# A GRU scan over four directions: the border exchanged in four pieces, and fourteen homes for the last tiles

## The reference

```
seq = gn(x) @ Wi.T + bi                  # 192 -> 64 channels per pixel
r = sigmoid(xr + hr); z = sigmoid(xz + hz); n = tanh(xn + r * hn)
h_new = (1 - z) * n + z * h              # 128 steps along rows or columns
out = hs @ Wo.T + bo                     # 64 -> 192 channels
result = x + (right + down + left + up) / 4
```

## Time and profile before

| | |
|---|---|
| median of three runs | 2590.5 us (2584.61 to 2591.54) |
| profiled execution: own time, span | 2584.67 us, 2582.6 us |
| granted TensorE clock, mean | 0.989 |
| busy share of the span | TensorE 87%, VectorE 79%, ScalarE 62%, GpSimd 59% |
| DMA, mean over the span | 197 GB/s, 509.23 MB |

### The profile page before, as it was taken

The page is one execution under the profiler, slowest core; times in us unless marked ns, Lnnn a source line. Parts: engine busy times, 40 slices in busy tenths (PEclk is TensorE's granted clock), DMA queues, the critical chain, the costliest instruction groups (busy, mean ns, idle before and its releaser), DMA issues.

```text
span 2582.6 us, 79658 instructions
## 1 busy us (share of the span) xinstructions
PE 2255.1 (87%) x30544; PEld 1419.1 (55%) x30544; DVE 2053.0 (79%) x4910; ACT 1602.1 (62%) x3374; POOL 1534.0 (59%) x2108
## 2 busy tenths in 40 slices
PE   0679999999979999898979999899979999999886
PEld 0345555555546655555546665555546666555564
DVE  8239999777769999787859999788857777898854
ACT  0236666666657777666647777666657777666600
POOL 2026666667756666566656666566667766666600
PEclk9999999999989999999989999999999999999999
DMA  9973333246768786589977776589974544244299
GB/s 364 276 213 94 99 94 87 79 133 207 244 196 232 209 228 181 157 241 281 311 249 204 216 233 173 156 248 278 308 228 127 129 130 116 79 127 129 60 381 390
DMA packets 331354, 509.23 MB, mean 197 GB/s; under 512 B 36704, under 2 KB 145632, under 8 KB 330208
## 3 DMA queue, kind: packets, MB, share of 16 engines
q1 hardware_dynamic: 313248, 478.28, 63.3%
q10 hardware_dynamic: 17728, 25.85, 2.7%
HBM read 352.98 MB, written 151.01 MB: 195 GB/s over the span
## 4 chain that ended last, share of the span: by engine, by line
PE 38%; ACT 21%; DVE 20%; issue 12%; DMA 5%; SPq 4%; POOL 0%; DVEq 0%; POOLq 0%
PE bank L776 23%; ACT bank L585 8%; DVE r L896 7%; ACT z L581 6%; ACT r L577 6%; PE bank L756 5%; DVE h L910 5%; DMA work<-x 4%; PE bank L684 4%; DVE bank L901 4%; SPq L326 3%; PE bank L777 3%; DVE r L891 2%; PE bank L758 1%; DVE bn L1021 1%
## 5 line engine op out<-in xcount | busy, mean ns | idle before, releaser
L776 PE MATMUL bank<-h,wh 64*64 64x256 f32 x6144 | 1510.3, 384 | 120.1 <-DVE h L910 119.4
L756 PE MATMUL bank<-seq,wx 64*64 64x256 f32 x6144 | 1551.0, 385 | 62.6 <-DMA seq<-seq_next 23.2
L758 PE MATMUL bank<-seq,wx 64*64 64x256 f32 x6144 | 1551.8, 385 | 0.0
L777 PE MATMUL bank<-h,wh 64*64 64x256 f32 x6144 | 1518.4, 386 | 0.5 <-issue 0.5
L475 POOL TENSOR_TENSOR v<-z,h 128x256 f32<-128x256 f32 x1024 | 747.6, 730 | 782.9 <-ACT z L581 780.5
L776 PEld LDWEIGHTS bank<-h,wh 64*64 64x64 f32 x6144 | 730.4, 133 | 519.5 <-PE bank L758 301.1
L756 PEld LDWEIGHTS bank<-seq,wx 64*64 64x64 f32 x6144 | 742.1, 132 | 361.9 <-DVE r L896 210.9
L483 POOL TENSOR_TENSOR hsum<-hsum,h 128x256 f32<-128x256 f32 x1024 | 751.6, 734 | 101.1 <-DVE h L910 79.3
L758 PEld LDWEIGHTS bank<-seq,wx 64*64 64x64 f32 x6144 | 740.8, 132 | 13.9
L891 DVE SCALAR_TENSOR_TENSOR r<-bank,bhh,r 128x256 f32<-128x256 f32 x1024 | 491.4, 480 | 321.4 <-ACT r L577 268.4
L777 PEld LDWEIGHTS bank<-h,wh 64*64 64x64 f32 x6144 | 731.8, 133 | 0.1
(11 more groups left out here) (97 smaller groups left out, 2468.0 us busy)
## 6 DMA issues: line engine op xcount, KB each, us to landing
work<-x SPq DMA_DIRECT2D x832, 128.0 KB, 3.9
work<-x SPq DMA_DIRECT2D x192, 384.0 KB, 4.2
out<-work SPq DMA_DIRECT2D x576, 128.0 KB, 2.5
work<-x SPq DMA_DIRECT2D x128, 512.0 KB, 5.4
work<-x SPq DMA_DIRECT2D x32, 768.0 KB, 6.2
seq_next<-work SPq DMA_DIRECT2D x48, 512.0 KB, 5.9
work<-hsum_last SPq DMA_DIRECT2D x48, 512.0 KB, 6.0
seq<-x SPq DMA_DIRECT2D x32, 512.0 KB, 14.4
```

What stands on the lines that cost most here:

```text
L756: pe.matmul(as_pair(ps[LOW, :], c), wx[HIGH, gate, :], px[HIGH], start=start, stop=False, skip_group_check=True)
L758: return pe.matmul(as_pair(ps[HIGH, :], c), wx[LOW, gate, :], px[LOW], start=start, stop=False, skip_group_check=True)
L776: pe.matmul(ps[LOW, 0:N2], wh[LOW, gate, :], state[LOW], start=start, stop=True, skip_group_check=True)
L777: return pe.matmul(ps[HIGH, 0:N2], wh[HIGH, gate, :], state[HIGH], start=start, stop=True, skip_group_check=True)
```

## The change

At each seam the border is split in four pieces, i = 0 to 3: rows 8 to 15 of the blocks 1 to 7 (448 KB), rows 16 to 127 of block 0 (896 KB), rows 0 to 15 of block 0 (128 KB), rows 0 to 7 of the blocks 1 to 7 (448 KB). Each has its own semaphores and waits for the step that leaves it (`BORDER_STEPS`). Piece 0 is fetched from step 125 on; all four are dumped ahead of the next pair's chunk loads. GpSimd starts a pair with its first two products and clears the pieces between them and the first additions, which move back. TensorE waits for the pieces 1 and 2 before the first product of c = 0, and for 0 and 3 before that of c = 1. At the end, `xe` has fourteen slots: the three of `xp`, rows 32 to 127 of each of the eight blocks of `seq`, and the three of `xf`. Ten tiles are loaded during the last recurrence, in the steps of `xe_at`: three at steps 0 to 2, six at 113 to 118, one at 121.

```diff
-    TSLOTS = 10
+    TSLOTS = 14
+    EDGE = 32
...
-    PIECES = sum(len(square_pieces(k)) for k in range(4))
+    PIECES = sum(len(square_pieces(k)) for k in range(3))
+    BORDER = [(slice(1, NB), slice(8, 16)), (slice(0, 1), slice(16, HH)), (slice(0, 1), slice(0, 16)),
+              (slice(1, NB), slice(0, 8))]
+    BORDER_STEPS = [(120, 124), (T, 120), (T, T), (T, T)]
+    FIRST_BORDER_AT = 125
...
-    clear_after = [(slice(0, 1), slice(0, HH)), (slice(1, NB), slice(0, 16))]
-    CLEARS = len(clear_at) + len(clear_after)
+    CLEARS = len(clear_at) + len(BORDER)
...
-        xe = seq[:, :, :, :].rearrange("p b r w -> p (b r w)")[:, 0:TSLOTS * XW]\
-            .rearrange("p (s k n) -> p s k n", s=TSLOTS, k=3)
+        assert (HH - EDGE) * BW == XW
+        xe = [xp[:, s] for s in range(XPS)]
+        xe += [seq[:, b, EDGE:HH, :].rearrange("p r w -> p (r w)").rearrange("p (k n) -> p k n", k=3)
+               for b in reversed(range(NB))]
+        xe += [xf[:, s] for s in range(XFS)]
+        assert len(xe) == TSLOTS
+        last_read = [max(T - 1 - BW // 2 * b, T - 1 - EDGE // 2) for b in reversed(range(NB))]
+        xe_at = {}
+        for s in range(XPS):
+            xe_at.setdefault(s, []).append(s)
+        for s, step in enumerate(last_read):
+            if step < T - 1:
+                xe_at.setdefault(step + 2 + (s if step + 2 + s < T and s < 6 else 0), []).append(XPS + s)
...
+            def fetch_border(g, i):
+                for c in range(2):
+                    sp.wait_ge(x_z_ready[c], T * g + BORDER_STEPS[i][c])
+                stored = TILES // 2 * (g + 1) - (i == 0)
+                for a in range(2):
+                    sp.wait_ge(stage_stored[a], 16 * ((stored + 1 - a) // 2))
+                blocks, rows = BORDER[i]
+                sp.dma_start(seq[:, blocks, rows, :], seq_next[:, blocks, rows, :]).then_inc(border_fetched[i], 16)
+            def dump_border(g, i):
+                for c in range(2):
+                    sp.wait_ge(h_added[c], T * g + BORDER_STEPS[i][c])
+                blocks, rows = BORDER[i]
+                sp.dma_start(hsum_last[g % 2][:, blocks, rows, :], hsum[:, blocks, rows, :])\
+                  .then_inc(border_dumped[i], 16)
...
+            def load_last(i):
+                s = i % TSLOTS
+                if i >= TSLOTS:
+                    sp.wait_ge(xe_stored[s], 48 * (i // TSLOTS))
+                elif s < XPS:
+                    sp.wait_ge(xp_used, TILES * (PAIRS - 1))
+                elif s < XPS + NB:
+                    for c in range(2):
+                        sp.wait_ge(x_z_ready[c], T * (PAIRS - 1) + last_read[s - XPS] + 1)
+                else:
+                    k = s - XPS - NB
+                    sp.wait_ge(xf_stored[k], 96 * ((TILES * (PAIRS - 1) + XFS - 1 - k) // XFS))
+                load_x(xe[s], PAIRS - 1, i, xe_loaded[s])
...
-                if last:
-                    dump_hsum(g - 1, 3)
...
+                    if not more and t in xe_at:
+                        for i in xe_at[t]:
+                            load_last(i)
+                            issued.append(i)
+                    if more and t == FIRST_BORDER_AT:
+                        fetch_border(g, 0)
                 if more:
-                    fetch_seq(g, 3)
+                    for i in (1, 2, 3):
+                        fetch_border(g, i)
+                    for i in (1, 0, 2, 3):
+                        dump_border(g, i)
             for i in range(TILES):
-                s = i % TSLOTS
-                if i < TSLOTS:
-                    for c in range(2):
-                        sp.wait_ge(x_z_ready[c], T * PAIRS)
-                else:
-                    sp.wait_ge(xe_stored[s], 48 * (i // TSLOTS))
-                load_x(xe[:, s], PAIRS - 1, i, xe_loaded[s])
-            for s in range(XFS):
-                stored = TILES * (PAIRS - 1)
-                sp.wait_ge(xf_stored[s], 96 * ((stored + XFS - 1 - s) // XFS))
+                if i >= TSLOTS or i not in issued:
+                    load_last(i)
...
+            def clear_border(g, i):
+                pool.wait_ge(border_dumped[i], 16 * g)
+                clear(*BORDER[i])
...
+                make_v(g, 0, 0)
+                make_v(g, 0, 1)
                 if g > 0:
-                    pool.wait_ge(hsum_dumped[3], 16 * len(square_pieces(3)) * g)
-                    for blocks, rows in clear_after:
-                        clear(blocks, rows)
+                    clear_border(g, 1)
+                make_v(g, 1, 0)
+                if g > 0:
+                    for i in (0, 2, 3):
+                        clear_border(g, i)
                 pool.wait_ge(hsum_cleared, NB + CLEARS * g)
-                for t in range(T):
+                add_h(g, 0, 0)
+                make_v(g, 1, 1)
+                add_h(g, 0, 1)
+                add_h(g, 1, 0)
+                make_v(g, 2, 0)
+                add_h(g, 1, 1)
+                make_v(g, 2, 1)
+                add_h(g, 2, 0)
+                add_h(g, 2, 1)
+                for t in range(3, T):
...
                     pe.wait_ge(seq_fetched, 16 * PIECES * g)
+                    for i in (1, 2):
+                        pe.wait_ge(border_fetched[i], 16 * g)
                 x_r(g, 0, 0)
...
+                    if g > 0 and t == 0:
+                        for i in (0, 3):
+                            pe.wait_ge(border_fetched[i], 16 * g)
                     x_r(g, t, 1)
```

17 lines of the change are left out of this document (11 added, 6 removed).

## The result

| | before | after |
|---|---|---|
| median of the runs (lowest to highest) | 2591.0 us (2584.61 to 2592.79), 4 runs | 2543.4 us (2540.8 to 2546.15), 4 runs |
| profiled execution: own time, span | 2584.67, 2582.6 us | 2543.53, 2541.7 us |
| DMA, mean over the span | 197 GB/s, 509.23 MB | 200 GB/s, 509.24 MB |

The ratio is 0.9822, with a 95% interval of 0.9809 to 0.9835: faster by 1.8%, 2542.0 forecast and 2543.4 measured. The bytes are the same, so what has changed is when they move and who waits for them.

A forecast was written before the change was run, and what follows sets the result against it. It took the end to be bound by bytes and the seams by three waits in a row. Seams 26.2 plus end 18.4, 44.6 us off 2584.67, gave 2540.1, or 2545.9 from the median; it said 2542, range 2529 to 2557.

The forecast's parts named there:

- A: At the seams, TensorE starts once block 0's pieces land, idling 2.8 us at each; gain 14.8 us in all.
- B: At the seams, first products v go ahead of every clear, so VectorE's wait for the first h goes; gain 14.7 us.
- C: From first to second h at the seams, TensorE's second cold start goes; gain 3.7 us.
- The first cold start: TensorE's slow-clock start at each seam: whether it goes couldn't be read; nothing taken, at most 1.5 us a seam.
- D: At the seams, clears between GpSimd's products make v(1,1) late; loss 1.5 us a seam, 4.5 in all.
- E: At the seams, new waits for piece 3 and the first chunk; loss 1.0, 1.0 and 0.5, 2.5 us in all.
- F: In the end phase, ten of 32 tiles already loaded save 19.4 us, less 1 charged; gain 18.4, bounds 14 and 20.4.
- G: In the last recurrence, the early tile loads delay nothing; cost 0, up to 3 us without cover.
- half-as-good seams: Rival: piece 3, first chunk and first finishing unit make engines wait; seams give 16.7, total 2549 to 2555 us; chance 0.17.
- the rival with the poor end: Rival: the end's remaining bytes go at 355 GB/s, taking 120 us, so the end gives 4: 2554 us; chance 0.08.

The follow-up runs named there:

- clears_first: The changed kernel, but GpSimd clears all four border pieces before its first product of a pair; 2556.1 us, 0.9874 of the kernel before.
- products_first: The kernel before, with only GpSimd's order changed: three products ahead of the wait for the dump and the undivided clears; 2576.7 us, 0.9962.
- chunks_ahead: The changed kernel, with the four chunk loads again ahead of the dumps, behind the fetches; 2547.3 us, 0.9842 of the kernel before.
- two_store_queues: The changed kernel, but SyncE issues the end's stores of tiles 25, 27, 29 and 31; 2546.2 us, 0.9844 of the kernel before.
- five_early: The changed kernel, with five of the end's tiles loaded during the last recurrence instead of ten; 2550.2 us, 0.9862 of the kernel before.
- one_chunk_between: The changed kernel, with the first chunk load between fetches and dumps and the border's large piece waiting for one store less; 2539.0 us, 0.9811.
- two_chunks_early: The changed kernel, with two chunk loads right behind the last store of seq_next, ahead of the fetches; 2542.1 us, 0.9820 of the kernel before.
- dump_ahead: The kernel before, with only the border's dump, in two parts as before, moved ahead of the four chunk loads; 2575.5 us, 0.9953.

## Why the prediction was right

**A, TensorE's start: 14.8 forecast, 13.3 measured.** 7.45 - 2.98, 7.28 - 2.69 and 8.49 - 4.28. Only the third idle is far from the 2.8 that I gave each.

**B, the first h: 14.7, and 14.7 measured.** None waits. In `clears_first`, where only GpSimd's order is undone, 10.8 us of waiting for the first v are back, and a cold start behind each. `products_first` shows that the order without the rest passes 3 us at each seam on to v(1,1). The dumps' place ahead of the chunk loads is not what earned it (`chunks_ahead`: 0.3 us in all).

**C, the second cold start: 3.7 forecast, 2.7 measured.** From first to second h it is now 4.28, 5.06 and 4.11 us once the chunk's waits are taken out, where it was 5.78, 6.28 and 4.12: 1.50 + 1.22 + 0. At the second seam a cold start has come back: the chunk's wait left TensorE idle for 3.50 us, and it went on at 0.50. The sum had the cold start and the chunk as separate terms; here one made the other.

**The first cold start: nothing taken, 1.6 gained.** The stretch from last to first h fell by 10.24, 13.33 and 5.98 us; A and B explain 11.22, 10.72 and 6.01. The rest is -1.0, +2.6 and 0, and it follows the clock. Windows of the first seam, before:

```profile
738.20:739.20 1.00, 1.00 (x18) 0.81 (x12) 0.00 (x0) 0.47 (x1) 0.00 (x0) 0.66 1.04 439
```

After:

```profile
738.20:739.20 1.00, 1.00 (x14) 0.76 (x12) 0.08 (x1) 0.62 (x2) 0.54 (x1) 0.50 0.98 212
739.20:740.20 1.00, 1.00 (x18) 0.53 (x10) 0.49 (x2) 0.75 (x3) 0.19 (x1) 0.98 0.95 278
```

TensorE began at 735.23 and at 733.21, so that the lower level lasted some 3.6 us behind its start before and 6.0 after. At the second seam it was 5.4 and nothing, at the third 5.2 and 5.5. Half of such a stretch is lost: 1.2 more at the first seam, 2.7 less at the second, 0.1 more at the third (estimates, from windows of 1 us). The bound of 1.5 a seam was too low, and it had no room for a cold start that grows.

**D, the clears: 4.5 forecast, 2.8 measured.** From second to third h it is now 4.85, 4.91 and 5.53 us. Before it was 4.20, 4.19 and 4.11 (the stretches of the table less the pairs in the earlier trace rows), so 0.65, 0.72 and 1.42 more. At the third seam, where nothing else delays VectorE, the value of 1.5 held; at the others it was half of that, and at the second a part of it belongs to the cold start behind the chunk's wait. C and D err by 1 and 1.7 us in opposite directions.

**E, new waits: 2.5 forecast, 4.3 measured,** 0.62 + 3.68, all for chunk 0. It lands 10.7 to 11.0 us after the last h in each kernel with this queue, where I had placed it at 736 to 738.5, some 8 to 10 after. So it is a floor: at the second seam the warm restart brought the first h to 6.65, and the wait took 3.68 of it again. The gain of 1.6 and this 4.3 are therefore one term, a loss of 2.7 against the 2.5 of the sum.

Seams: 13.3 + 14.7 + 2.7 + 1.6 - 2.8 - 4.3 = 25.2, as measured; forecast 26.2.

**F, the end: 18.4 forecast, 16.75 measured in this execution, and this is the term that was mis-sized.** Eight profiled executions with the ten early tiles have ends of 113.96 to 118.66, mean 116.4; five without them 129.7 to 131.2, mean 130.7. So on average F is 14.3, at the lower end of its bounds (14 to 20.4). I had valued the bytes at 405 GB/s, 19.4 us, and charged 1 us for the start. Counted against 405 (estimates from windows), the old end loses 6.5 us: 4.2 in its first 22 us and 2.4 in the 8.0 behind VectorE's last tile. The new end loses 9.3: 4.3 in its first 22 us, 0.2 in the middle, and 4.8 in the tail of 23.4 us behind the last tile. 19.4 less 2.8 is 16.6, about what was measured. So the start costs nothing new, and what I left out is the tail: VectorE is not bound by loads any longer, ends early, and only stores are left. In the six executions with ten early tiles that took longer (115.6 to 118.7, without `two_store_queues`), the tail loses 3.8 to 6.2 us and the middle runs at 387 to 402 GB/s, 0.5 to 3.3 us lost; why it is slower in them stays open. I had looked for the lost bytes at the beginning of the phase and not at its end. `five_early` shows the same tail, and `two_store_queues` that a second queue doesn't mend it; what limits stores alone stays open.

**G, the early loads' cost: 0, and 0.** 519.9 against 520.0 us for the last recurrence.

**Rivals.** The half-as-good seams needed D and E at 7.5 and 9; they were 2.8 and 4.3. Piece 3 with its 512 B rows held nobody: TensorE's rows show one wait for a fetch at each seam, that before its first product. The rival with the poor end had a part: F came nearer to its lower bound than to my value, by the tail, not by the mix of reads and writes, which kept 405 in this execution. That rival was also mispriced: it set 120 us at 355 GB/s against 124.3 at 405, but the old end took 130.7, with its slow start, so 355 would still have given some 11 us and not 4. The fixed 2 us for each DMA, which the prediction takes from the Trainium skill, stands there (DMA: Bandwidth & Descriptors, Anatomy of one DMA — SWDGE (gpsimd) path) for DMAs issued by GpSimd, which none of these pieces is. It would be paid by each small piece waited for alone. Such a cost could hide in the 4.28 us of the third start, where I had 2.8; no run tells it apart, and the cut as a whole gained. The same skill (Perfetto Trace Analysis, Roofline) says that a single active core can go beyond 358 GB/s, to about 120% of it; the 405 of this trace is 113% and agrees.

That the median came within 1.4 us of the forecast owes something to chance: from the profiled execution's own time the sum was 2540.1, 3.4 below its 2543.53, and the 2 that I added for the median, where the runs' offset was 6, cancelled most of that. Nor do the rows account for the whole difference of the medians: the profiled pair differs by 40.9 us of the 47.6, since the profiled execution of the kernel before (2584.67) lies at its fastest run. And the 16.75 of the end is 2.4 more than F gives on average.

## What to carry to other kernels

When a block must go out and another come in between two stages, cut it by who needs which part first, and order the one queue by the time at which each piece is wanted (no run here tests the cut apart from the order); a piece wanted by two engines at nearly the same time is worth trying in both places, since at the second seam 3.7 us hung on one chunk load. A product that needs nothing of the block belongs ahead of the clear, but part of the wait moves on to the next product (alone it gave 5.9 us at two seams and lost 1.0 at the third). For a phase bound by bytes, count what is left at its mean rate, with its ends: loads taken out of it leave a longer tail in which nothing but stores runs.

## What the runs showed of the hardware that I had not expected

- Loads and stores together ran at 405 GB/s, stores alone at 388 and then 324 to 331, and two queues for them made no difference (366, then 287).
- TensorE's restart after a short idle can be at either level of its clock, and the length of the idle alone doesn't tell which: 0.50 after 2.98 us in the kernel after, 1.00 after 2.88 in `clears_first` (both at the first seam), and in `one_chunk_between` 1.00 at the third seam after 3.39. The first matmul doesn't tell either: in `two_chunks_early` it took 0.40 us after an idle of 3.97, and the window that begins 1.5 us later shows 0.50; in `clears_first`, third seam, it is 1.00 in the first us and 0.54 in the next. The clock can fall when the engine is already at work again. From TensorE's start to the first h went 4.7 us at the second seam of the changed kernel, at the full clock, and 7.6 and 7.3 at the others.
- Pieces of 128 to 896 KB, with 512 B rows in some, queued one behind another showed no cost for being small: all four dumps, 1.97 MB, were down 9.8 us after the last h at the first seam (the last was issued at 734.3 and landed 6.5 us later); in `dump_ahead`, where two DMAs carry the same bytes, also behind the fetches and ahead of the chunks, it was 12.2 (there the whole border is fetched ahead of them, here a part of it, 448 KB, goes out earlier).
